# Self-attention of a transformer block: both halves of a value product ahead of the second half's transposes, and the two groups of output products one behind the other

## The reference, cut to what matters

```
h1 = layernorm(x) * (1 + scale) + shift
q, k, v = h1 @ wq, h1 @ wk, h1 @ wv            # 16 heads of 64
out = softmax(q @ k.T / 8) @ v                 # per head, 112 x 112
x = out.reshape(112, 1024) @ wo + bo + x
h2 = ...; x = cross attention of h2 over ctx (375 rows, own k2 and v2) + x
x = gated feed-forward(...) + x
```

## Time and profile before

| What | Value |
|---|---|
| Median of 3 runs | 3028.2 us (3027.29, 3028.2, 3032.8) |
| Span of the profiled execution, first to last instruction | 2885.4 us |
| Median less span: what lies around the span | 142.8 us |
| PE busy | 2750.6 us (95%), 18151 matmuls |
| DVE busy | 1512.9 us (52%), 4453 instructions |
| ACT busy | 1094.4 us (38%) |
| Mean granted clock of PE | 0.985 |
| One turn of the loop over the samples | 82.4 us |

### The profile page before, as it was taken

The page is one execution under the profiler, slowest core; times in us unless marked ns, Lnnn a source line. Parts: engine busy times, 40 slices in busy tenths (PEclk is TensorE's granted clock), DMA queues, the critical chain, the costliest instruction groups (busy, mean ns, idle before and its releaser), DMA issues. The chain is left out here.

```text
span 2885.4 us, 61782 instructions
## 1 busy us (share of the span) xinstructions
PE 2750.6 (95%) x18151; PEld 1862.3 (65%) x18152; DVE 1512.9 (52%) x4453; ACT 1094.4 (38%) x2869; POOL 899.8 (31%) x1692
## 2 busy tenths in 40 slices
PE   7999999999999999998799988999999999999798
PEld 5777766777777667776455545556555566565597
DVE  4455555455455554555566655555555555544432
ACT  1434343334343433343266633344333343333332
POOL 0012221221122212211444535534344444440343
PEclk9999999999999999999899999999999999999899
DMA  6000000000000000001677750100001000000251
GB/s 228 7 10 9 9 9 9 9 3 5 9 9 9 9 9 9 3 6 48 191 226 233 218 148 23 40 25 21 21 21 37 27 21 21 21 21 7 92 175 26
DMA packets 87764, 145.65 MB, mean 50 GB/s; under 512 B 22402, under 2 KB 64383, under 8 KB 86160
## 3 DMA queue, kind: packets, MB, share of 16 engines
q1 hardware_dynamic: 44304, 84.85, 9.2%
q0 software_dynamic: 20848, 41.09, 5.4%
q10 hardware_dynamic: 22544, 18.89, 2.0%
HBM read 116.17 MB, written 29.51 MB: 50 GB/s over the span
## 5 line engine op out<-in xcount | busy, mean ns | idle before, releaser
L952 PE MATMUL psG<-W,ctxT 128*125 128x512 f32 (+2 forms) x896 | 408.5, 599 | 4.9 <-DVE v L2578 4.9
L1577 ACT ACTIVATE probs<-psG,nmax 112x375 f32<-112x375 f32 (+1 forms) x512 | 317.0, 620 | 252.0 <-DVE nmax L1987 252.0
L946 PE MATMUL psG<-ctxT,W 128*128 128x375 f32 (+1 forms) x1024 | 386.9, 525 | 2.0 <-ACT ctxT L1798 1.1
L1987 DVE TENSOR_REDUCE nmax<-psG 112x1 f32<-112x375 f32 (+1 forms) x512 | 284.9, 601 | 121.0 <-PE psG L894 116.7
L911 PEld LDWEIGHTS psT<-ident,probs 112*125 112x125 f32 (+2 forms) x1792 | 201.7, 167 | 157.1 <-ACT probs L1577 110.4
L946 PEld LDWEIGHTS psG<-ctxT,W 128*128 128x128 f32 x1024 | 188.9, 189 | 162.9 <-issue 106.8
L940 PEld LDWEIGHTS psG<-hT,W 128*128 128x128 f32 x2304 | 269.2, 195 | 24.9 <-ACT hT L1604 16.2
L940 PE MATMUL psG<-hT,W 128*128 128x112 f32 x2304 | 279.6, 280 | 3.2 <-ACT hT L1604 3.2
L952 PEld LDWEIGHTS psG<-W,ctxT 128*125 128x125 f32 (+2 forms) x896 | 159.4, 186 | 178.6 <-issue 170.7
L911 PE MATMUL psT<-ident,probs 112*125 112x112 f32 (+2 forms) x1792 | 248.9, 276 | 19.8 <-ACT probs L1577 15.9
L894 PE MATMUL psG<-kT,qT 64*112 64x375 f32 (+1 forms) x1024 | 243.9, 563 | 1.1 <-DVE v L2578 0.6
(11 more groups left out here) (382 smaller groups left out, 4282.3 us busy)
## 6 DMA issues: line engine op xcount, KB each, us to landing
W<-in_ew SPq DMA_DIRECT2D x64, 384.0 KB, 4.2
expert_rows<-W ACTq DMA_DIRECT2D x144, 128.0 KB
W<-in_ew SPq DMA_DIRECT2D x8, 2048.0 KB, 10.9
ctxT<-in_ctxT SPq DMA_DIRECT2D x16, 375.0 KB, 3.2
kT<-in_ctx SPq DMA_DIRECT2D x16, 375.0 KB
normed_rows<-hrow SPq DMA_DIRECT2D x32, 112.0 KB, 1.9
W<-normed_rows,ids POOLq DMA_INDIRECT x144
slot_table<-stt,st POOLq DMA_INDIRECT x136, 2.1
```

Of the source, the lines that this page charges most:

```text
L946: mm = nc.tensor.matmul(bank[:, 0:n], wt[:, c, n0 + j * P:n0 + (j + 1) * P], src[:, c, 0:n], start=(c == 0), stop=(c == DC - 1))
L952: mm = nc.tensor.matmul(bank[0:kn, 0:512], src[:, c, k0:k0 + kn], wt[:, c, n0 + half * 512:n0 + (half + 1) * 512], start=(c == 0), stop=(c ...
L1577: nc.scalar.activation(probs[:, 2 * (s % 2) + i, 0:keys], psG[0:T, score_banks(s)[i], 0:keys], ACT.Exp, bias=nmax[:, h:h + 1], accum_out=r ...
L1987: nc.vector.tensor_reduce(nmax[:, 2 * s + i:2 * s + i + 1], psG[0:T, score_banks(s)[i], 0:keys], AXX, ALU.max, negate=True).then_inc(max_r ...
```

## The change

On PE, side 1 of the value product moves up beside side 0; the second half's two transposes follow; then the spreading of the first half's reciprocals, and both halves' output products. On DVE, the copy of side 1 moves up from behind `self_invert(1)` to a place ahead of `self_copy(2)`. ACT's list, POOL's and SP's stay as they are. Nothing is added or removed.

```diff
                 self_turn(1)
                 self_scores(1)
                 pe.wait_ge(w_in["v2"], 16)
-                values2(0, True, (0,))
+                values2(0, True)
+                self_turn(2)
+                self_turn(3)
+                spread_half(spreadA, 0, psG[:, 1, :])
                 self_outputs(0)
-                self_turn(2)
-                spread_half(spreadA, 0, psG[:, 1, :])
-                self_turn(3)
-                values2(0, True, (1,))
                 self_outputs(1)
                 spread_half(spreadA, 1, psT[:, 1, :])
...
                 chain(self_sum(1))
                 self_invert(0)
+                values2(0, True)
                 self_copy(2)
                 self_sum(2)
                 self_copy(3)
                 chain(self_sum(3))
                 self_invert(1)
-                values2(0, True)
```

## The result

The kernel after takes 3038.99 us (median of 7 runs, 3037.34 to 3043.34), the kernel before 3030.42 us in its 7 runs beside it: 1.003 of the time before, 95% interval 1.002 to 1.0041. That is 8.6 us more, and 6 to 12 us by the interval. The forecast was +4.8 us and 3033.0 us, with a range up to 3037.5.

The account below looks back on a forecast made before the run. PE's list was taken to bound the loop, with DVE as tight in the edited stretch. A slip of 0.30 us in each of 16 batches gave +4.8 us on 3028.2, so 3033.0 us, range 3028 to 3037.5.

Parts of the forecast that it names:

- PE's wait on probsT: Self-attention, before the second half's output products: PE waits some 0.4 us for DVE's second probsT copy, 16 times.
- the one on the reciprocals: Self-attention, before spreading half 1's reciprocals (L846): PE waits some 0.45 us for DVE, 16 times.
- the path: From `self_scores(1)` to `project_out` on PE: 9.05 us where it was 8.75, +0.30 us a batch.
- The sum, 16 x 0.30: Same slip of 0.30 us in all 16 batches: +4.8 us, giving 3033.0 us, +0.16%.
- The 142.8 us around it are left alone: Whole kernel: the span of 2885.4 us becomes 2890.2; the 142.8 us between span and median run time stay unchanged.
- The bounds: Self-attention slip: +7.8 us with release times and copy cost all against the edit, +3.8 us with all in its favour.
- PE's release by DVE: At the two new waits in self-attention: PE follows DVE by 0.04 us; at 0.15, `project_out` comes at 313.06.
- the faster one: Self-attention: PE's list decides, grouping saves changes of shape, -0.52 us a batch, -8.3 us, 3019.9 us; chance 0.12.
- The slower one: Self-attention: longer releases or dearer v2 copy, +0.38 to +0.56 a batch, +6.1 to +9 us; chance 0.30.
- No change: The slip is taken up by a later wait, or oT alone holds `project_out`: 3028.2 us; chance 0.08.
- the 0.7 us wait: PE's gap before the routing's rank product each loop turn, on DVE; said to slip too, not absorb the delay.
- The rule of the Trainium skill: Matmuls should run back to back because the engine scales power by use; said to gain nothing, loop clock being 1.00.

Follow-up runs that it names:

- grouped_late_copy: Kernel before with PE's new order, and on DVE the copy of v2 moved behind both products into oT: ratio 1.0018, 4.9 us more than before.
- pe_only: Kernel before with PE's new order alone, DVE keeping its old order: ratio 1.0061 to the kernel before, 17.8 us between the medians.
- padded: Kernel before with one more copy on DVE, result unused, behind the second reciprocals: ratio 1.0009 to the kernel before, 1.9 us more.
- late_copy: Kernel before with PE untouched and DVE's copy of v2 moved behind both products into oT: ratio 0.9977 in both runs, 7.0 and 5.9 us faster.
- before_again: Kernel before, no edit, run again for a second profile: ratio 1.0007, span 3041.6 us, its execution 3043.44 us.

## Why the prediction was wrong, point by point

- *What bounds the stretch, and the cost of each part: right.* PE's wait on probsT was forecast at 0.4 and is 0.30, the one on the reciprocals 0.45 and 0.37, L962's wait about zero and zero, the path 9.05 and 9.03 us. Loop turns without stalls go from 82.39 to 82.66 us. The sum over the samples: sample 0 gives 0.27, the 14 turns 0.27 each, and the last 9.43 against 8.85 us to the projection, 0.58; 4.6 us, forecast 4.8. (In the last one DVE takes 0.70 instead of 0.31 from the reciprocals to their spreading, and PE waits 0.77 in front of L846. That the sum came out close owes a little to this.) The mechanism (a copy nobody needs yet, ahead of four steps for which PE waits) is shown by grouped_late_copy and pe_only, which differ from the change only in where that copy stands: 8.82 and 9.41 us.
- *The step that failed: that nothing outside the self-attention changes.* The sum, 16 x 0.30, took the stretch as the whole and put every other stage at nothing, without a reason; neither bound has a term for them. On the two chips without stalls the change costs 9.7 and 8.6 us: 4.6 in the self-attention and 3 to 4 in the expert stretch, where PE meets a new wait in front of L1327, 9 to 11 times; the rest is within the scatter of two medians. The cause of that wait stays open. Excluded by runs are the last sample's order and the 0.2 us slip of padded. Not excluded are the place of PE's instructions, a start of the stretch later than 1497.6 us, and the place of DVE's copy.
- *The comparison with 3030.42 us ran on chips with the stalls,* and there the runs do not show where the missing time lies. The three comparisons of the kernels before and after give 6.4 to 13.5 us by the medians, and the expert stretch does not differ. So of the 8.6 us some 4 have no place yet. A turn of the loop takes 89.5 and 89.7 us on average in two profiles of the old order and 90.0 to 90.3 in four of the new, a difference of 0.3 to 0.8 where the slip is 0.28. The 130 matmuls in which the stalls lie take 20.3 and 20.1 us in the two profiles, and 20.3, 20.6, 20.6 and 20.5 in the four. Some 0.3 over 14 turns would be the missing 4 us, but single turns scatter by 0.7, and late_copy, with the old order on PE, has 20.3 and 20.5. Whether the change adds something there is not settled.
- *"The 142.8 us around it are left alone": wrong as a fact.* They are inside the span, most of them as stalls and 1.2 GHz stretches. The term cancels in the difference, but it hid that the profile and the timed runs came from chips on which this program runs differently: the granted clock over the loop is 0.96 in the profiles of before_again and after, not the 1.00 of the earlier trace rows.
- *The bounds* held for the stretch (+3.8 to +7.8 us). The value of 0.04 us for PE's release by DVE was about right, 0.15 too long: the copy L1935 ends at 327.11 and L846 starts at 327.16.
- *The rivals:* the faster one is excluded by grouped_late_copy, where even with the copy out of the way the new order is 0.07 us a turn slower than the old. The slower one named the size (+6.1 to +9, measured +8.6), but that is luck, since its mechanism is not what happened: the releases were short, and the path is 9.03 us as in the forecast. *No change* did not happen; the 0.7 us wait is 0.7 in all profiles, it slipped as said.
- *The rule of the Trainium skill* weighed there ("Perfetto Trace Analysis", "Matmul Optimizations") gave nothing here: the clock on the chips without stalls is 1.00 in the loop with both orders. On the chips with them the trace agrees that idle places go with a lower clock (0.83 over the 19.6 us of the stretch above), but the new order did not take them away.

## What to carry to other kernels

Moving a product to an earlier place on the engine that sets the time also moves its copy on the engine behind it, and that copy should then go to where nobody waits on what follows it, not to where its input comes in. Here the copy alone, moved behind the last urgent step, gives 6 to 7 us where the whole reordering costs 8.6. And a span that lies far from the measured time is no margin around it: the difference has to be found before a change is added to it. A stage that an edit does not touch still needs a reason for being put at nothing. And an edit that is to shift instructions by one is to be counted in the trace: here an added wait shared an instruction that was there, and shifted none.

## What was not expected of the hardware

- The same program takes 2886.7 to 2887.1 us on three chips and 3033.0 and 3038.6 us on two others (medians). In the profiles of before and before_again, 102.7 of the 156.2 us between the spans are in the 14 turns of the loop: some 3 us a turn in which PE gets no instruction to run, always 46 to 54 us behind the first scores, and in all but one turn of nine profiles 3 to 10 us at 1.2 GHz behind it. Sample 0, written out ahead of the loop, has neither. What stops PE was not found. Transfers of instructions (queues q8 and q14) do not coincide with it: in before_again none starts between 211 and 1401 us.
- Code inside one loop changes the time of a later, unchanged loop by 3 to 4 us of 180, reproducibly over three chips, with the same clock and nearly the same busy times. It is a wait without a partner at one fixed matmul of the later loop's turn, and in every profile without stalls it goes with a loop body on PE that is one instruction shorter. On the chips with the stalls every profile has this wait.
- Two waits can share one instruction of PE's list, so a wait more or less in the source need not move the code behind it (4282 and 4296 such instructions, unchanged by either edit).
